# Four chained transformer layers on one core: softmax sums moved from TensorE to GpSimd and VectorE, masks as 64x64 tiles a pair ahead, and another order within the slot

## The reference

```
Q, K, V = split_heads(q @ wq + bq), split_heads(k @ wk + bk), split_heads(v @ wv + bv)
scores  = where(mask == 0, -1e20, Q @ K.T / sqrt(DK))        # 64 x 64 per head
out     = (softmax(scores) @ V) @ wo + bo
```

## Time and profile before

| | before |
|---|---|
| median of 3 runs | 814.97 us (814.9 to 818.01) |
| the profiled execution | 817.6 us |
| its span, first to last instruction | 815.8 us |
| TensorE busy | 708.1 us (87%) |
| VectorE busy | 531.0 us (65%) |
| ScalarE busy | 445.2 us (55%) |
| GpSimd busy | 304.5 us (37%) |
| mean granted TensorE clock | 0.944 of full speed |

### The profile page before, as it was taken

One profiled execution on the slowest core, in us unless ns is written; L12 is line 12 of the kernel. 1 busy time (PEld: TensorE's weight loads), 2 busy tenths in 40 slices (PEclk: granted clock), 3 DMA queues, 4 the chain that ended last, 5 costly groups with the idle time before them and its releaser, 6 DMA issues.

```text
span 815.8 us, 26360 instructions
## 1 busy us (share of the span) xinstructions
PE 708.1 (87%) x9248; PEld 471.6 (58%) x9248; DVE 531.0 (65%) x1329; ACT 445.2 (55%) x1242; POOL 304.5 (37%) x497
## 2 busy tenths in 40 slices
PE   2999999999999999999977977777724789999996
PEld 1565666777766666666654755555522456666774
DVE  0698888888888877788872422222222566888784
ACT  1466666766667777777653232222202434676884
POOL 2244444566665333326666100000036663443110
PEclk9999999999999999999986999999975767999998
DMA  8333333223233111111100101111112110111110
GB/s 252 85 79 82 86 81 83 54 60 89 81 91 104 31 28 34 35 27 47 41 22 36 36 26 41 39 42 40 30 39 63 44 39 22 31 30 29 47 42 27
DMA packets 61085, 44.85 MB, mean 55 GB/s; under 512 B 18240, under 2 KB 55488, under 8 KB 59840
## 3 DMA queue, kind: packets, MB, share of 16 engines
q1 hardware_dynamic: 56592, 27.42, 12.0%
q10 hardware_dynamic: 2352, 12.00, 6.0%
q0 software_dynamic: 2048, 4.20, 1.6%
HBM read 22.68 MB, written 14.61 MB: 46 GB/s over the span
## 4 chain that ended last, share of the span: by engine, by line
PE 66%; issue 14%; POOL 7%; DVE 6%; ACT 3%; DMA 1%; ACTq 1%; SPq 0%; POOLq 0%; DVEq 0%
PE ps L560 10%; PE ps L602 9%; PE ps L784 5%; PE ps L722 4%; PE ps L793 4%; PE ps L578 4%; PE ps L655 3%; DVE hid_t L1264 3%; PE ps L730 3%; PE ps L643 3%; PE ps L677 3%; POOL k_by_j L485 2%; PE ps L802 2%; PE ps L587 2%; PE ps L750 2%
## 5 line engine op out<-in xcount | busy, mean ns | idle before, releaser
L1065 DVE TENSOR_REDUCE top<-ps 128x16 f32<-128x1024 f32 (+1 forms) x96 | 108.9, 1134 | 67.7 <-PE ps L560 66.9
L560 PE MATMUL ps<-k_by_j,q_t 32*64 32x256 f32 (+1 forms) x1536 | 126.7, 401 | 0.4 <-issue 0.2
L602 PE MATMUL ps<-cst,prob 128*128 128x128 f32 x704 | 122.3, 295 | 0.8 <-ACT prob L920 0.7
L477 POOL TENSOR_TENSOR rstd<-spread,half_neg 128x1 f32<-128x1 f32 x80 | 44.3, 553 | 207.5 <-DVE spread L1157 119.2
L485 POOL TENSOR_TENSOR k_by_j<-k_t,cst 128x512 f32<-128x512 f32 (+1 forms) x96 | 94.8, 988 | 71.9 <-ACT k_t L901 36.8
L602 PEld LDWEIGHTS ps<-cst,prob 128*128 128x128 f32 x704 | 78.5, 146 | 62.6 <-issue 59.2
L1080 DVE TENSOR_TENSOR prob<-ps,top 128x1024 f32<-128x1024 f32 (+1 forms) x96 | 108.8, 1134 | 0.7
L920 ACT ACTIVATE prob<-prob 128x1024 f32<-128x1024 f32 (+1 forms) x96 | 94.8, 987 | 20.3 <-DVE prob L1080 19.4
L1031 DVE RECIPROCAL inv<-ps 128x128 f32<-128x128 f32 x96 | 91.6, 954 | 11.7 <-PE ps L730 7.8
L518 POOL DMA_INDIRECT got<-expert_out,source x32 | 30.8, 963 | 158.8 <-DMA expert_out<-rows_out 150.2
L1264 DVE COPY hid_t<-ps 128x512 f32<-128x512 f32 x39 | 27.0, 691 | 95.0 <-PE ps L802 95.0
(11 more groups left out here) (160 smaller groups left out, 1287.9 us busy)
## 6 DMA issues: line engine op xcount, KB each, us to landing
sorted_rows<-zero_rows ACTq DMA_DIRECT2D x32, 272.0 KB, 2.7
stage_x<-x_t SPq DMA_DIRECT2D x80, 64.0 KB, 1.8
mow<-in_mow SPq DMA_DIRECT2D x18, 256.0 KB, 3.1
stage_kv<-in_ctx_t SPq DMA_DIRECT2D x64, 64.0 KB
stage_m<-in_m SPq DMA_DIRECT2D x80, 32.0 KB, 1.9
rows_in<-sorted_rows SPq DMA_DIRECT2D x39, 64.0 KB, 1.8
expert_out<-rows_out SPq DMA_DIRECT2D x39, 64.0 KB, 1.5
wat<-in_wat ACTq DMA_DIRECT2D x1, 1280.0 KB, 6.5
```

The costliest lines, as they stand in the source:

```text
L560: mm = pe.matmul(ps[S * b:S * b + S, 2 * p + bank, r * nj * S:(r + 1) * nj * S].rearrange("p (h k) -> p h k", k=S), q_t[rows_g, p, S * b:S ...
L602: mm = pe.transpose(ps[:, 2 * p + half, k * 128:(k + 1) * 128], prob[:, p, q * 128:(q + 1) * 128], ident)
L1065: dve.tensor_reduce(top[:, p, 0:nh].rearrange("p (b h) -> p b h", b=2), sc, AX.X, ALU.max).then_inc(top_d, 1)
```

## The change

- The softmax sums leave TensorE. GpSimd adds the two halves of every row of 64 exponentials (`halves`, 128x1024 to 128x512), VectorE sums the 32 left (`total`), takes 16 reciprocals per token (`inv_h`) and spreads them to 128x128 (`inv`). TensorE turns that tile (`rt_d`), ScalarE evacuates it (`inv_t`, `rt_e`), and VectorE multiplies by it where it multiplied by the reciprocal of the sums.
- The masks are four 64x64 tiles of 512 columns in place of two 128x128 matmuls, and are done one slot before the scores (`mask_d`). For that each row of the mask holds its own and its partner's 64 columns: the mask's load and its conversion are twice as wide.
- `OFF_FT` = 8 is a new offset: the feed-forward's transposition and residual come a slot later, so its norms move to offsets 9 and 10.
- On PE the output projection stands between the two score rounds, both ahead of the transpositions, and is no longer behind the projections. On DVE `y` and the statistics stand ahead of the row maxima. On POOL `k_by_j` moves a slot later, to the head of the slot, with the halves behind it and everything else after them.
- v is evacuated in two instructions per pair where there were four.

The core of the diff:

```diff
+OFF_FY, OFF_FT, OFF_FN, OFF_FB = 7, 8, 9, 10
 OFF_R1, OFF_R2, OFF_RP, OFF_RS = 6, 7, 8, 9
...
+                pr = at(OFF_V)
+                if pr is not None:
+                    p, nj = pr.p, heads(pr) // 4
+                    cj = C_J16 if nj == 4 else C_J8
+                    wait_pair(pool, k_e, pr)
+                    wait_pair(pool, score_d, pr, 2)
+                    pool.tensor_tensor(k_by_j[:, p, 0:nj, :], k_t[:, p:p + 1, :].broadcast_to([128, nj, TOK]),
+                                       cst[:, cj:cj + nj].unsqueeze(2).broadcast_to([128, nj, TOK]), ALU.mult)\
+                        .then_inc(kj_d, 1)
+
+                pr = at(OFF_PV)
+                if pr is not None:
+                    p, nh = pr.p, heads(pr)
+                    keys = prob[:, p, 0:nh * S].rearrange("p (h k) -> p h k", k=S)
+                    wait_pair(pool, exp_d, pr)
+                    wait_pair(pool, sum_d, pr, 2)
+                    pool.tensor_tensor(halves[:, p, 0:nh * S // 2].rearrange("p (h k) -> p h k", k=S // 2),
+                                       keys[:, :, 0:S // 2], keys[:, :, S // 2:S], ALU.add).then_inc(half_d, 1)
                 pr = follows(at, OFF_FN, FF)
...
-                pr = at(OFF_PROJ)
-                if pr is not None:
-                    p, nj = pr.p, heads(pr) // 4
...
-                    pool.tensor_tensor(k_by_j[:, p, 0:nj, :], k_t[:, p:p + 1, :].broadcast_to([128, nj, TOK]),
-                                       cst[:, cj:cj + nj].unsqueeze(2).broadcast_to([128, nj, TOK]), ALU.mult)\
-                        .then_inc(kj_d, 1)
...
                 pr = at(OFF_SCORE)
                 if pr is not None:
-                    p = pr.p
+                    wait_pair(pe, pt1_e, pr, 2)
                     if MASKED[pr.phase]:
-                        wait_pair(pe, neg_d, pr)
-                    wait_pair(pe, pt1_e, pr, 2)
+                        wait_pair(pe, mask_d, pr)
                     wait_pair(pe, q_e, pr)
                     wait_pair(pe, kj_d, pr)
-                    if MASKED[pr.phase]:
-                        for bank in range(2):
-                            pe.matmul(ps[:, 2 * p + bank, :].rearrange("p (h k) -> p h k", k=S), idb[:, :],
-                                      neg_m[:, p:p + 1, :].broadcast_to([128, 8, S]), start=True, stop=False,
-                                      skip_group_check=True)
                     score_round(pr, 0).then_inc(round_d, 1)
+
+                pr = at(OFF_OUT)
+                if pr is not None:
+                    wait_pair(pe, heads_d, pr)
+                    wait_pair(pe, xt_e, pr, 2)
+                    wait_pair(pe, y_d, pr, 1)
+                    before = follows(at, OFF_FB + 1, FF)
+                    if before is not None:
+                        wait_own(pe, f_xt, before)
+                    before = follows(at, OFF_FT + 1, FF)
+                    if before is not None:
+                        wait_own(pe, f_y, before)
+                    done = follows(at, OFF_FT, FF)
+                    if done is not None:
+                        wait_own(pe, f_o, done)
+                        pe.transpose(ps[:, B_OUT, TURN], sum_f[:, done.p, :], ident).then_inc(f_turn, 1)
+                    pe.matmul(ps[:, B_OUT, OUT], heads_t[:, pr.p, :], wat[:, pr.phase, 3, :], start=True, stop=True)\
+                        .then_inc(out_d, 1)
+
+                pr = at(OFF_SCORE)
+                if pr is not None:
+                    score_round(pr, 1).then_inc(score_d, 1)
 
                 pr = follows(at, OFF_FY, FF)
...
+                        wait_pair(pe, rt_e, turned, 1)
                     wv = wat[:, ph, 2, :].rearrange("c (h par d) -> c par h d", par=2, d=dk)
                     for b in range(2):
...
+                pr = at(OFF_PV)
+                if pr is not None:
+                    wait_pair(pe, inv_d, pr)
+                    wait_pair(pe, rt_e, pr, 1)
+                    if at(OFF_V) is None:
+                        pe.wait_ge(v_e, NP * (pr.phase + 1))
+                    pe.transpose(ps[:, B_PROJ, 384:512], inv[:, pr.p, :], ident).then_inc(rt_d, 1)
...
+                pr = at(OFF_V)
+                if pr is not None:
+                    p = pr.p
+                    if MASKED[pr.phase]:
+                        wait_apart(pe, neg_d, pr.n + 1)
+                        wait_pair(pe, pt1_e, pr, 2)
+                        for bank in range(2):
+                            for b in range(2):
+                                rows_m = slice(S * (b ^ bank), S * (b ^ bank) + S)
+                                mm = pe.matmul(ps[S * b:S * b + S, 2 * p + bank, :].rearrange("p (h k) -> p h k", k=S),
+                                               idb[rows_m, rows_m], neg_m[rows_m, p, bank:bank + 1, :].broadcast_to([S, 8, S]),
+                                               start=True, stop=False, skip_group_check=True)
+                        mm.then_inc(mask_d, 1)
 
...
-
-                    for k in range(step):
-                        for g in range(4):
-                            half, c = divmod(g * step + k, npr // 2)
-                            mm = pe.matmul(ps[32 * g:32 * g + 32, B_HEADS, 128:128 + TOK], own_ones(pr, k),
-                                           prob_t[:, p, half, c * 128:c * 128 + TOK],
-                                           start=k == 0, stop=k == step - 1, skip_group_check=True)
...
+            def evacuate_inverse(pr):
+                wait_pair(act, rt_d, pr)
+                wait_pair(act, heads_d, pr, 2)
+                act.activation(inv_t[:, pr.p, :], ps[:, B_PROJ, 384:512], ACT.Copy).then_inc(rt_e, 1)
...
                     p = pr.p
                     wait_pair(act, proj_d, pr)
+                    turned = at(OFF_PV)
+                    if turned is not None:
+                        evacuate_inverse(turned)
...
                     p = pr.p
+                    wait_pair(dve, rt_e, pr)
                     wait_pair(dve, pv_d, pr)
-                    wait_pair(dve, heads_d, pr, 2)
-                    dve.reciprocal(inv[:, p, :], ps[:, B_HEADS, 128:128 + TOK]).then_inc(inv_d, 1)
                     wait_pair(dve, out_d, pr, 2)
-                    wait_pair(dve, inv_d, pr)
-                    dve.tensor_tensor(heads_t[:, p, :], ps[:, B_HEADS, 0:TOK], inv[:, p, :], ALU.mult)\
+                    dve.tensor_tensor(heads_t[:, p, :], ps[:, B_HEADS, 0:TOK], inv_t[:, p, :], ALU.mult)\
                         .then_inc(heads_d, 1)
...
+                pr = at(OFF_PV)
+                if pr is not None:
+                    p, nh = pr.p, heads(pr)
+                    wait_pair(dve, half_d, pr)
+                    wait_pair(dve, inv_d, pr, 2)
+                    dve.tensor_reduce(total[:, p, 0:nh], halves[:, p, 0:nh * S // 2].rearrange("p (h k) -> p h k", k=S // 2),
+                                      AX.X, ALU.add).then_inc(sum_d, 1)
+
+                pr = at(OFF_PV)
+                if pr is not None:
+                    p, nh = pr.p, heads(pr)
+                    wait_pair(dve, sum_d, pr)
+                    wait_pair(dve, inv_d, pr, 2)
+                    dve.reciprocal(inv_h[:, p, 0:nh], total[:, p, 0:nh]).then_inc(rcp_d, 1)
+                pr = at(OFF_PV)
+                if pr is not None:
+                    p, nh = pr.p, heads(pr)
+                    wait_pair(dve, rcp_d, pr)
+                    wait_pair(dve, rt_d, pr, 2)
+                    dve.tensor_copy(inv[:, p, :].rearrange("p (h d) -> p h d", h=nh),
+                                    inv_h[:, p, 0:nh].unsqueeze(2).broadcast_to([128, nh, D // nh])).then_inc(inv_d, 1)
+
+                pr = at(OFF_SCORE)
+                if pr is not None:
+                    p, nh = pr.p, heads(pr)
...
                 pr = at(OFF_PROJ)
                 if pr is not None and MASKED[pr.phase]:
                     p = pr.p
                     dve.wait_ge(ld_m[p], 16 * (pr.half + 1))
...
+                    wait_pair(dve, mask_d, pr, 2)
+                    dve.tensor_scalar(neg_m[:, p, :, :], stage_m[:, p, :].rearrange("p (a k) -> p a k", a=2), 0, None, ALU.is_equal)\
+                        .then_inc(neg_d, 1)
 
...
+
+
+def both_ways(mask):
+
+    m = mask.reshape(NP, 2, S, S)
```

186 lines of the change are left out of this document (81 added, 105 removed).

## The result

The changed kernel takes 922.58 us (median of 4 runs, 919.11 to 923.63), the kernel before on the same chip 815.6 us: ratio 1.130, 95% interval 1.126 to 1.134. The profiled execution took 923.1 us with a span of 921.2. The forecast was 908 us, between 868 and 943.

The account below looks back on a forecast made before the run. TensorE bounded the plain slots; with the change, a chain from one inverse to the next would. Terms 10 + 47 + 12 + 27 + 1 - 4 = +93 us on 817.6 gave 910.6, less 2.6 to the median: 908 us, range 868 to 943.

Parts of the forecast that it names:

- the term behind the experts: First four slots of the second pipeline: room for halves, shorter wait through the earlier projection, -4 us, between -12 and +6.
- the idle times and their releasers: Expected in the profile: VectorE idle until GpSimd releases norms or sums, TensorE idle before the turned inverse in plain slots.
- the squares at 0.8 us or more: Expected in the profile: the sum of squares L1113 takes 0.8 us or more in phases 2 and 3.
- Halves, 1.25 us: On GpSimd, adding 512 sums of two arrays was priced at 1.25 us, between 1.06 and 1.47.
- Feed-forward slot, 10.6 us: Chain through exponentials, halves, powers and norms to the next inverse: 10.6 us against 7.77, +40 for fourteen slots.
- the first rival: The forecast plus a falling TensorE clock in feed-forward slots, little in the router's: +20, 928 us, chance 0.20.
- Router slot, 9.35 us: Loop through GpSimd's `chosen`, scatters, `k_by_j` and halves to the next inverse: 9.35 us against 6.39, +27 for nine slots.
- for which the sums wait: 8.1: Step in the router slots: `k_by_j` and halves follow the scatters, so the sums can start at 8.1 us.
- RMS slots, 6.25 us, +12: Sixteen RMS slots without scatter: the halves hold up the sum of squares, 6.25 us against 5.5, +12.
- Plain slots, 5.9 against 5.5, +10: 26 plain slots: chain from one inverse to the next of 5.9 us against 5.50, +10.
- Masks, 0.33: On TensorE, four 64x64 mask tiles side by side take some 0.33 us, where the masks took 0.54.
- The rivals of a faster kernel and of no change: TensorE stays the bound, about 778 us, chance 0.06; tiles not side by side or plain chain 5.5, 815 us, chance 0.03.

Follow-up runs that it names:

- e6: The changed kernel with unused matmuls added on TensorE ahead of two waits in the feed-forward slots: 918.9 us.
- e1: The changed kernel with the two powers of the feed-forward's norms ahead of `k_by_j` and the halves on GpSimd: 877.3 us.
- e2: The changed kernel with the router's two scatters ahead of `chosen` and `taken` in GpSimd's queue: 902.8 us.
- e5: The changed kernel with the sum of squares in RMS and router slots replaced by a maximum reading `y` once: 912.7 us.
- e4: The changed kernel without the halves on GpSimd, VectorE summing all 64 keys of a head itself: 899.1 us.
- e3: The changed kernel with the transposition of the inverse behind the masks and the product with v on TensorE: 924.8 us.
- e7: The kernel before with the mask part of the change alone: 807.9 us, ratio 0.982.
- e13: e12 with `k_by_j` made for the pair one slot older, early in the slot instead of at its end: 795.0 us, ratio 0.971.
- e12: The kernel before with the masks as 64x64 tiles and v evacuated in two instructions instead of four: 803.5 us, ratio 0.977.
- e11: The changed kernel with five queue orders mended (powers, scatters, squares, turned inverse, `normed`): 850.8 us, ratio 1.036.
- e10: e3 with `normed` made ahead of `heads_t` on VectorE as well: 948.8 us.

## Why the prediction was right, and where its sum was off

- **The signs and places** all held: every stretch moved in the foretold direction. 922.6 lies 14.6 above the 908, inside the range. The sum was 93, the measured difference 105.5. Part of that nearness is luck: the term behind the experts gained 10.2 us more than forecast, and all the other stretches together cost 22.7 more. Of the signs named ahead, the idle times and their releasers are there; the squares at 0.8 us or more came in 14 of their 32 executions only.
- **Halves, 1.25 us.** The form of 512 takes 1.27 (the mean of 1.18 holds those of 256 in phase 5).
- **Feed-forward slot, 10.6 us.** With the clock held up in e6 it is 10.61. The chain was right step by step, and e1, which breaks it at the one place, takes it away. What was left out of the sum is the clock: +6.8 us here. That was the first rival, priced at +20 and given 0.20; its mechanism was real, its size a third. The truth was forecast and rival together, between their two times. The rival held its cost in the router's slots for little; the clock is 0.58 there, and no run shows what that costs.
- **Router slot, 9.35 us.** Measured 9.7. The step that does not hold in every slot is "for which the sums wait: 8.1": it let the 1.14 us of maxima pass beside `k_by_j` and halves. In four of the nine slots the sum of squares stands ahead of them and is held up until the halves end, so the maxima come behind; the hold-up had been costed in the RMS slots and forgotten here. It is not all of the 3.4 us: the slot ahead of the one shown, whose squares take 0.29 us, takes 10.16 us against its 10.68. How the rest divides between hold-up and clock stays open. That the loop runs through GpSimd is shown by e2.
- **RMS slots, 6.25 us, +12.** Measured +14.8. Where the slots run evenly they take 6.01 us, and 5.34 without the hold-up (e5): the forecast had 0.8 us of hold-up on a chain of 5.45, it is 0.67 on one of 5.34. Twelve of the sixteen slots give 6.2 us together; the other 8.6 are in the first, the fifth and the last two, which the sum did not tell apart, and why these lose 1.9 to 2.5 us each was not tried. So the mechanism was right, and the nearness of +12 is luck.
- **Plain slots, 5.9 against 5.5, +10.** Measured 6.07 against 5.53, and +13.9 for the 26. Fifteen of the first 17 take 5.93 in the mean, where they took 5.53: the forecast's 0.4. The other 3.4 us of the 9.4 are in two slots at the start, of 6.44 and 7.77 us; in the longer one the eight matmuls of L623 take 1.97 us, after 1.09 in the slot ahead, the low clock again. That it was the chain, and that VectorE's sums stand on it, is shown by e4 (0.54 us more in the median slot for 0.55 more of sums). That it hangs on masks and product behind the transposition is so in part: e3 took them out of the chain and gained 0.28 of the 1.0 us, for then VectorE's own queue, with a held-up `normed`, and the way over the projection took its place. Against the same slots of the changed kernel e3 gained 0.3 us where `normed` was not held up, and nothing in the two that start at 126.94 and 132.69, where it was.
- **Masks, 0.33.** Measured 0.34, and as a pure gain in e7.
- **Behind the experts, -4 (between -12 and +6).** Measured -14.2, outside the term's bounds. The step looked at the halves and at the earlier projection, and not at `k_by_j`, which the change moves past the gathers' place too: its 9.8 us of waits stood ahead of them. e13, which changes this order alone against e12, shows it.
- The rivals of a faster kernel and of no change had their condition named: a feed-forward chain under 7.2 us and a plain one under 4.9. e11, with five orders mended, has 7.7 and 6.0; the shortest plain slots of e3 take 5.4.

## What to carry to other kernels

A cheap instruction is priced by what stands behind it in its queue. The halves cost GpSimd 1.2 us a slot, which it had; the kernel lost 107 us because two powers, two scatters, a sum of squares and a chain of four engines came to be tied to them. Before moving work off the busiest engine, write down the loop that this closes, from one use of the result to the next, and compare it with the slot's length: with five queue orders mended the kernel was still 3.6% slower than the one before. And take a change apart: three of its parts (mask tiles, v in two copies, `k_by_j` a slot later) made the kernel before 2.9% faster, beneath a whole that was 13% slower.

## What the runs showed of the hardware that had not been expected

- A VectorE instruction in conflict with GpSimd may wait for more than one of its instructions: the squares at 483.79 us began beside a scatter, 0.25 us ahead of `k_by_j`, and ended at 486.47, behind `k_by_j` and halves, which followed each other without a gap.
- `normed`, with one full array from SBUF and two columns of one element as scalars, is held up as well: 1.08 us beside `k_by_j` (e3), 0.82 in the changed kernel, 0.34 while GpSimd is idle (e10). The same section of the Trainium skill (SBUF — State Buffer, "Who interferes with whom") lists `tensor_scalar` among the forms that can contend, and the trace agrees.
- A lead of 0.04 us more decided which of the two waits. In e3 `normed` took 0.34 us in every plain slot in which it started 0.08 us or more ahead of `k_by_j`, 1.16 us in the eight in which it started 0.04 ahead, and 1.08 in the three in which it started 0.04 behind. At a lead of 0.08 us `k_by_j` took 1.16 us in place of 1.04: then GpSimd waits.
- Four unused matmuls per slot raised the granted clock from 0.80 to 1.00 and made the kernel's feed-forward slots 4% faster. That gain comes from a TensorE that waits 0.9 to 2.2 us at a stretch in most of these slots; where it has no such gaps nothing of the kind was tried.
